# Mixture-of-experts rows sorted by single expert, or by pair of experts

## What is computed

```python
logits = einsum('bsd,de->bse', input, Wg)          # input is layernorm(x)
top_vals, top_idx = top_k(softmax(logits), 2)
top_vals = top_vals / sum(top_vals)
h = relu(einsum('ebsd,edh->ebsh', xm, W1) + b1)    # 8 experts, 128 -> 256
y = einsum('ebsh,ehd->ebsd', h, W2) + b2           # 256 -> 128
out = sum over the token's two experts of y * its share
x = x + layernorm(out)
```

## Time and profile before

| | |
|---|---|
| median of 3 runs | 952.27 us |
| profiled execution | 948.08 us |
| its span, first to last instruction | 946.2 us |
| busy: PE, DVE, ACT, POOL | 779.7, 751.3, 684.6, 581.6 us |
| mean granted TensorE clock | 0.938 |

### The profile page before, as it was taken

The page is one execution under the profiler, slowest core; times in us unless marked ns, Lnnn a source line. Parts: engine busy times, 40 slices in busy tenths (PEclk is TensorE's granted clock), DMA queues, the critical chain, the costliest instruction groups (busy, mean ns, idle before and its releaser), DMA issues.

```text
span 946.2 us, 24562 instructions
## 1 busy us (share of the span) xinstructions
PE 779.7 (82%) x7544; PEld 647.1 (68%) x7544; DVE 751.3 (79%) x2293; ACT 684.6 (72%) x1596; POOL 581.6 (61%) x832
## 2 busy tenths in 40 slices
PE   3699999999999999999999999986784798848700
PEld 2487877877877777777777777765774687738600
DVE  5677879898998989989899899977854565647876
ACT  4678888887887778877888778752663597739744
POOL 4344434376766757666676666665777777777722
PEclk9999999999999999999999999996797899989955
DMA  7000000000000000000000000062232543364643
GB/s 203 18 2 5 4 3 5 3 18 18 16 18 16 19 16 16 19 18 17 16 20 16 18 17 18 18 170 68 82 90 77 140 110 100 96 207 126 170 134 116
DMA packets 64817, 53.04 MB, mean 56 GB/s; under 512 B 11127, under 2 KB 58515, under 8 KB 64688
## 3 DMA queue, kind: packets, MB, share of 16 engines
q1 hardware_dynamic: 55600, 34.40, 13.5%
q0 software_dynamic: 9088, 17.07, 5.6%
HBM read 26.70 MB, written 25.50 MB: 55 GB/s over the span
## 4 chain that ended last, share of the span: by engine, by line
PE 48%; DVE 16%; issue 10%; ACT 7%; DMA 7%; SPq 5%; POOL 5%; DVEq 1%; POOLq 0%; ACTq 0%
PE bank L859 6%; PE bank L656 5%; PE bank L931 4%; PE bank L658 4%; PE bank L657 4%; POOL expert_results L2025 3%; PE bank L843 3%; PE bank L845 3%; PE bank L914 2%; PE bank L877 2%; PE bank L920 2%; DMA expert_results<-moe_y,moe_dest 2%; SPq L1654 2%; DMA rows<-csplit 2%; PE bank L870 2%
## 5 line engine op out<-in xcount | busy, mean ns | idle before, releaser
L2025 POOL DMA_INDIRECT expert_results<-moe_y,moe_dest x156 | 157.6, 1010 | 49.8 <-issue 42.9
L1305 POOL DMA_INDIRECT expert_rows<-xall,row_index x128 | 138.7, 1084 | 30.9 <-issue 25.3
L1020 POOL TENSOR_TENSOR y<-y,zt 128x256 f32<-128x256 f32 x64 | 46.8, 731 | 140.2 <-issue 88.7
L943 ACT ACTIVATE m<-bank 128x512 f32<-128x512 f32 x128 | 69.2, 592 | 71.6 <-PE bank L845 71.6
L2000 PE MATMUL bank<-moe_w,moe_hid 128*128 x624 | 93.5, 297 | 30.7 <-DVE moe_y L2018 22.3
L656 PE MATMUL bank<-thi,whi 128*128 128x512 f32 x224 | 105.1, 469 | 8.5 <-ACT bt L697 4.4
L2000 PEld LDWEIGHTS bank<-moe_w,moe_hid 128*128 128x128 f32 x624 | 82.3, 205 | 37.5 <-issue 36.2
L1029 DVE TENSOR_TENSOR mg<-bank,m 128x512 f32<-128x512 f32 x128 | 82.4, 685 | 19.8 <-PE bank L859 19.1
L658 PE MATMUL bank<-thi,wlo 128*128 128x512 f32 x224 | 89.7, 401 | 0.0
L657 PE MATMUL bank<-tlo,whi 128*128 128x512 f32 x224 | 89.5, 400 | 0.0
L982 POOL TENSOR_TENSOR ysum<-ysq 128x128 f32<-128x128 f32 x64 | 35.6, 556 | 71.2 <-ACT ysq L966 71.2
(11 more groups left out here) (235 smaller groups left out, 2395.0 us busy)
## 6 DMA issues: line engine op xcount, KB each, us to landing
moe_block_in<-expert_rows SPq DMA_DIRECT2D x78, 132.0 KB, 2.2
rows<-expert_results SPq DMA_DIRECT2D x12, 512.0 KB, 5.1
out_dram<-m SPq DMA_DIRECT2D x16, 256.0 KB, 2.3
expert_results<-moe_y,moe_dest POOLq DMA_INDIRECT x156
expert_rows<-spare_row SPq DMA_DIRECT2D x18, 132.0 KB, 2.8
parts<-csplit SPq DMA_DIRECT2D x128, 4.0 KB
rows<-csplit SPq DMA_DIRECT2D x128, 4.0 KB
expert_rows<-xall,row_index POOLq DMA_INDIRECT x128, 2.5
```

Source lines behind the costliest of these rows:

```text
L943: SE.activation(m[:, hf * HH:(hf + 1) * HH, :], banks[2 + hf][:].rearrange("p (h l) -> p h l", l=P), ACT.Exp).then_inc(m_ready.sem, 1)
L1305: PL.indirect_dma_start(buckets[n], bass.IndirectOffsetOnAxis(row_index[:, k, t:t + 1], 0), xall[:, t, :], None).then_inc(scattered[n], 16)
L2025: PL.indirect_dma_start(back_d, bass.IndirectOffsetOnAxis(dest[:, b % BACK, n:n + 1], 0), yout[:, b % BACK, n, :], None, bounds_check=2 * ...
```

## The change

Each token's row goes once to a bucket of its *pair* of experts (28 pairs). A unit is 128 rows of one pair; both experts are computed on it, mixed, normalised, and added to x, and one finished row per token is written to the output by an indirect DMA. There are 91 units instead of 78 blocks of 256 rows, and no last pass. The first 20 units hold rows of groups 0 to 11 only (`SPLIT = 12`, `EARLY = 20`) and run beside the last groups' routing; a unit past the end of a pair takes rows again, and those are not written twice (`again`, `skip`).

For W1 a table of both experts' columns for each of 28 pairs (and one spare) is written to DRAM during groups 3 to 10; each unit loads its 128 x 516 floats. The products with W1 are plain float32 of 128 columns without the split in two parts.

```diff
-BLK = 2 * P
-SPLIT = 11
+NPAIR = NE * (NE - 1) // 2
+SPLIT = 12
+UNITS = (TOK + NPAIR * (P - 1)) // P                                      # 91
+EARLY = -(-(SPLIT * GT - NPAIR * (P - 1)) // P) // 4 * 4                  # 20
...
 def dve_route_second(dve, q):
-        DVE.tensor_tensor(chosen[:, 1], ranks, wide(rank2[:]), ALU.is_equal)
+        DVE.tensor_tensor(upper, rank1, rank2, ALU.max)
+        DVE.tensor_tensor(lower, rank1, rank2, ALU.min)
+        DVE.scalar_tensor_tensor(out=product, in0=upper, scalar=-1.0, in1=upper, op0=ALU.add, op1=ALU.mult)
+        DVE.scalar_tensor_tensor(out=number, in0=product, scalar=0.5, in1=lower, op0=ALU.mult, op1=ALU.add)
...
-        DVE.tensor_tensor(count16[:, :, 1:TG + 1].rearrange("p e t -> p t e"), chosen[:, 0], chosen[:, 1], ALU.add)
+        DVE.tensor_tensor(marks, pair_number ... [P, TG, NPAIR], number ... [P, TG, NPAIR], ALU.is_equal)
         DVE.tensor_tensor_scan(total16, chain16, count16, ...)            # 28 x 5 columns, was 8 x 5
 def dve_route_index(dve, q):
-        DVE.tensor_tensor(spot[:], chosen[:], at.to_broadcast([P, 2, TG, NE]), ALU.mult)
-            DVE.tensor_reduce(row_index[:, :, group(q)], spot[:], AX, ALU.add)
+        DVE.tensor_tensor(spot[:], count16[:, :, 1:TG + 1], at, ALU.mult)  # 28 x 4 columns
+        DVE.tensor_reduce(place[:], spot[:].rearrange("p e t -> p t e"), AX, ALU.add)
+        DVE.scalar_tensor_tensor(out=row_index[:, group(q)], in0=pair[:, 3, :], scalar=float(BUCKET), in1=place[:], ...)
+def pool_gap(pl, q):                      # 4 POOL instructions on 128x4, once a group, ahead of the first scatter
...
 def pool_body(...):
-        for q, n in plan("scatter", g, i):
-            pool_scatter(pl, q, n, 1)
+        if isinstance(t, int) and t == 8:
+            pool_pair_b1(pl)                                              # 15 small instructions
 def pool_tail(pl, step):                  # scatters at steps 0, 1, 6, 10 (were 0, 0, 2, 5)
 def sync_program(sp):
             for u in range(GB):
                 row_copies(sp, b, u)
+                sp_pair_weights(sp, (b - 1) * GB + u)
-        for rows_d in buckets:
-            sp.dma_start(rows_d[NE * BUCKET:NE * BUCKET + BLK].rearrange("(n p) c -> p n c", p=P), dummy[:])
+        for n in range(NPAIR + 1):
+            sp.dma_start(rows_d[n * BUCKET:n * BUCKET + P], dummy[:]).then_inc(spare_rows, 16)
...
     def act_prepare(act):
         act.wait_ge(loaded, LOADS)
-        SE.activation(w1[:, :, 0, :], w1f[:], ACT.Copy)
+        SE.activation(b2x[:], b2[:], ACT.Copy).then_inc(b2_act.sem, 1)
+        act.wait_ge(b2_dve.sem, 2)
+        SE.activation(b2x[64:P, :], b2[64:P, :], ACT.Copy).then_inc(b2_act.sem, 1)
+        act.wait_ge(b2_dve.sem, 3)
+        SE.activation(b2p[:].rearrange("p e d -> p (e d)"), b2[:], ACT.Copy).then_inc(b2_act.sem, 1)
     def dve_prepare(dve):                 # two differences of 1,024 columns, a wait, a third one
...
+    def pe_up(pe, u):
+        for n in range(2 * FB):
+            mm = PE.matmul(up_at(u)[:, col(n)], w1c[:, u % WR, col(n)], ht[:, (u // 2) % HT, col(u % 2)], ...)
+    def act_hidden(act, u):               # even units: 4 activations of 128 columns; dve_hidden: odd units
+    def pe_down(pe, u):
+        for k, e in enumerate(chosen.pop(u)):
+            o = down_at(u)[:, col(k)]
+            PE.matmul(o, thirds[:], b2p[:, bass.ds(e, 1), :] ..., start=True, stop=False)     # bfloat16: the bias
+            for n in range(FB):
+                mm = PE.matmul(o, hid[:, u % HID, k, n, :], w2[:, bass.ds(e, 1), n, :] ..., stop=n == FB - 1)
+    def dve_mix(dve, u):
+        DVE.tensor_scalar(y[:, u % YR, :], o[:, col(0)], w[:, 0, i:i + 1], None, ALU.mult)
+        DVE.scalar_tensor_tensor(out=y[:, u % YR, :], in0=o[:, col(1)], scalar=w[:, 1, i:i + 1], in1=y[:, u % YR, :], ...)
+        DVE.bn_stats(st6[:, u % YR, :], y[:, u % YR, :])
+        DVE.bn_aggr(mv[:, u % YR, :], st6[:, u % YR, :])
+    def pool_out(pl, u):
+        pl.wait_ge(normed.sem, normed.of(u))
+        PL.tensor_tensor(y[:, u % YR, :], y[:, u % YR, :], block_in[:, u % IN, 0:D], ALU.add).then_inc(added.sem, 1)
+        pl.wait_ge(added.sem, added.of(u))
+        PL.indirect_dma_start(rows_out, bass.IndirectOffsetOnAxis(token[:, u % IN:u % IN + 1], 0), y[:, u % YR, :], ...)
...
     def sync_program(sp):
+            for u in units[0:ROWS_AHEAD]:                                 # 5
+                sp_load(sp, u)                                            # 128 rows, start from the table
+            for u in units:
+                if u + ROWS_AHEAD in units:
+                    sp_load(sp, u + ROWS_AHEAD)
+                sp_pick(sp, u)                                            # 128 x 516 floats of the pair
     def gpsimd_program(pl):
+        for u in range(UNITS + NORM_LAG):                                 # NORM_LAG = 7
+            if u % 4 == 3 ...: pool_shares(pl, u // 4 + 1)                # 5 small instructions for 4 units
+            if u % 4 == 1 ...: pool_share_sums(pl, u // 4)                # 2
+            if u >= NORM_LAG:
+                pool_out(pl, u - NORM_LAG)
```

More of the change, by code:

```diff
@@ L376, in fr_uses @@
         for i in range(TG):
-            seq += [made(key) for key in EARLY[i]]
+            seq += [made(key) for key in SOON[i]]
             if g is not None:
@@ L1848, in after, with unit_of, dve_table @@
+    def unit_of(u):
+        return (0, u) if u < EARLY else (1, u - EARLY)
+    def dve_table(dve, n, half):
+        rows_of = att.rows_of[:, n, :]
+        pair_number, first_row = att.pair_number[:], att.first_row[:]
+        pid, first, wanted, low, high, product, lower, taken1, start, seen = [one[:, k:k + 1] for k in range(10)]
+        at = table_i[n]
         def after(step):
             dve.wait_ge(table.sem, table.of(n, step))
-        if part == 0:
+        if half == 0:
+            dve.wait_ge(att.rows_counted.sem, n + 1)
@@ new lines, in dve_table @@
+            if n == 0:
+                DVE.memset(begun[:], 0.0).then_inc(table.sem, 1)
+            after(5)
+            DVE.tensor_tensor_scan(ends[:], att.ones[:, 0:NPAIR], unit_rows[:], 0.0, ALU.mult, ALU.add
+                                   ).then_inc(table.sem, 1)
+            after(6)
+            DVE.tensor_scalar(past[:], ends[:], first_row, None, ALU.is_le).then_inc(table.sem, 1)
+            after(7)
+            DVE.tensor_reduce(pid, past[:], AX, ALU.add).then_inc(table.sem, 1)
@@ new lines, in dve_table @@
+            DVE.tensor_tensor(past[:], past[:], unit_rows[:], ALU.mult).then_inc(table.sem, 1)
+            after(9)
+            DVE.tensor_reduce(first, past[:], AX, ALU.add).then_inc(table.sem, 1)
+            DVE.tensor_scalar(mine[:], pair_number, pid, None, ALU.is_equal).then_inc(table.sem, 1)
+            after(11)
+            DVE.tensor_tensor(past[:], mine[:], taken[:], ALU.mult).then_inc(table.sem, 1)
+            after(12)
+            DVE.tensor_reduce(taken1, past[:], AX, ALU.add).then_inc(table.sem, 1)
@@ new lines, in dve_table @@
+            DVE.tensor_tensor(mine[:], mine[:], rows_of, ALU.mult).then_inc(table.sem, 1)
+            return
+        after(14)
+        DVE.tensor_reduce(high, mine[:], AX, ALU.add).then_inc(table.sem, 1)
+        DVE.scalar_tensor_tensor(out=wanted, in0=first_row, scalar=first, in1=taken1, op0=ALU.subtract, op1=ALU.add
+                                 ).then_inc(table.sem, 1)
+        DVE.tensor_scalar(tri_past[:], att.triangle[:], pid, None, ALU.is_le).then_inc(table.sem, 1)
+        after(16)
@@ new lines, in dve_table @@
+        DVE.tensor_scalar(wanted, wanted, float(P), None, ALU.add).then_inc(table.sem, 1)
+        DVE.tensor_scalar(high, high, -float(P), 0.0, ALU.add, ALU.max).then_inc(table.sem, 1)
+        after(19)
+        DVE.tensor_tensor(start, wanted, high, ALU.min).then_inc(table.sem, 1)
+        DVE.tensor_reduce(low, tri_past[:], AX, ALU.add).then_inc(table.sem, 1)
+        after(20)
+        DVE.scalar_tensor_tensor(out=at[:, 0:1], in0=pid, scalar=float(BUCKET), in1=start, op0=ALU.mult, op1=ALU.add
+                                 ).then_inc(table.sem, 1)
@@ L1981, in act_hidden @@
[L1981 to L1994 removed]
+        wait_picked(pe, u)
@@ new lines, in vector_program @@
+    def vector_program(dve):
+        dve_skip(dve, 0)
+        for u in range(UNITS + 4):
+            if u < UNITS:
+                att.dve_tail(dve, u)
+            if u in (11, 12):
+                dve_table(dve, 1, u - 11)
+            if u == 13:
+                dve_skip(dve, 1)
+            if u in COEF_AT:
+                dve_coef(dve, COEF_AT[u])
+            if u < UNITS and u % 2:
+                dve_hidden(dve, u)
+            if 2 <= u < UNITS + 2:
+                dve_mix(dve, u - 2)
+                if u - 2 in SPREAD_AT:
+                    dve_spread(dve, SPREAD_AT[u - 2])
```

1008 lines of the change are left out of this document (501 added, 507 removed).

## The result

The changed kernel takes **987.08 us** (median of 4 runs, 986.36 to 989.48) against 952.17 for the kernel before (4 runs): 1.0372 times as long, 95% interval 1.0353 to 1.0392. The forecast of 932, and its range to 962, were wrong. The profiled execution has a span of 987.6 us, where I had 926.5: 61.1 us to explain.

A forecast was written before the change was run, and what follows sets the result against it. It took TensorE to set the attention stage's pace, VectorE close behind, and GpSimd to bound the expert stage. Last pass -33, expert stage +3, 11 lost ahead: -19.7 from 952.3, forecast 932 us, range 905 to 962.

The forecast's parts named there:

- GpSimd's unit: Expert stage, GpSimd's work per unit: one indirect DMA 1.29, add 0.45, own wait 0.1, small steps 0.43, sum 2.27 us.
- 0.1 for its own wait: Expert stage, part of GpSimd's sum per unit: 0.1 us for its wait for its own step.
- The 2.4 per unit: Expert stage: 2.4 us per unit, between 2.15 (TensorE alone) and 2.27 + 0.5 for a late neighbour; 78 units make 187.
- Attention stage: Attention groups: +0.15 us each, between -0.6 and +1.2, over 13 groups: +2 us (-8 to +16).
- the forecast's +1.4: Attention stage: about +1.4 us of VectorE per group from added routing steps, longer scan and comparison, and the index.
- The relief by the missing scatters: Attention stage: four of eight scatters go, giving 0.8 us back per group, less four tiny GpSimd steps.
- the rival that rests on it: Attention stage: the routing costs its full VectorE work, +14 us, 946 us in all; chance 0.07.
- The head: Program start: eight more small loads, with 15 small GpSimd steps in tile 8, have idle time around them: 0, at most 2 us.
- The last group: End of attention: 29 spare-row DMAs (13.8 us) ahead of the weights' loads delay ScalarE's and VectorE's preparation: +9 us.
- The first units: First 13 units beside the last routing: 42.3 us as before, two units at 2.4, 5 for the longer table: 52.
- The end: After the unit loop: GpSimd drains seven units in 13 us, last landing and last unit's chain take 3.5 more.
- VectorE as the bound: Expert stage rival: VectorE, stretched by GpSimd, needs 3.0 us per unit, 47 us more, 979 us; chance 0.20.

The follow-up runs named there:

- The seven extra steps: Kernel before with seven chained VectorE operations of 128x4 elements put behind the running sum of each group's routing, results unchanged: 969.07 us, 1.0203.
- the late return: Changed kernel with each unit's return DMA issued one unit later, behind the next unit's add: 958.81 us, 1.0088 against the kernel before.

## Why the prediction was wrong

- **GpSimd's unit (the step that failed).** The term was "0.1 for its own wait". Together with the 0.28 of issue in the 1.29 per DMA that is 0.38 us ahead of the DMA, and 0.80 us pass there. No row stood behind the 0.1, and none could: the trace before has no GpSimd DMA behind a GpSimd operation that it waits for. The real sum is 1.01 + 0.80 + 0.46 + 0.43 = 2.70 instead of 2.27: 23.7 us in the loop, and 2.27 instead of 1.84 per unit in the drain, 3 us more. Taking the wait out gave back 28. With 0.80 in its place the same sum gives about 959 us, at the edge of the range to 962, so any second miss was enough to leave it.
- **The 2.4 per unit** came out at 2.39 without the wait, but in part by luck. It was a margin on 2.27 of GpSimd and 2.15 of TensorE; with the wait gone GpSimd is far from full, and TensorE, whose 2.15 was right (2.12 at full pace), loses 0.27 per unit in small delays.
- **Attention stage.** I took +0.15 per group from a range up to +1.2; it was the upper end: 12.7 us in groups 4 to 14, 0.9 in group 3. I had called TensorE (95%) the pace and VectorE (92%) a near second. But behind its wait for TensorE's scores in the first tile (0.93 to 1.09 us before, 0.39 to 0.78 after), VectorE has no gap over 0.04 us until the running sum of the decays in the fourth, and that decides when the split of the decays is done, for which the next group waits: a share of 92% hid a chain with little slack. The seven extra steps in the kernel before show that work in this chain counts. In group 8 VectorE reaches the running sum 31.13 us behind the group's start instead of 29.74. That these 1.39 are the forecast's +1.4 is luck, since they are made up otherwise. The routing's second part and the index cost 0.40 each, and its first part takes 0.31 less. The largest piece, 0.83, stands in five normalisation steps that the change does not touch (before, then after, then GpSimd beside them after):

```profile
346.65 1.38 DVE L1108 TENSOR_SCALAR ob<-ob,pmv,pt 128x128 f32<-128x128 f32 x4
348.06 1.28 DVE L1112 TENSOR_TENSOR xall<-ob,xall 128x512 f32<-128x512 f32 x1
```

```profile
355.77 2.38 DVE L1126 TENSOR_SCALAR ob<-ob,pmv,pt 128x128 f32<-128x128 f32 x4
358.18 1.12 DVE L1130 TENSOR_TENSOR xall<-ob,xall 128x512 f32<-128x512 f32 x1
```

```profile
357.33 0.60 POOL L1022 TENSOR_TENSOR decayed<-state,edec 128x256 f32<-128x256 f32 x1
358.03 0.71 POOL L1031 TENSOR_TENSOR zt<-zsig,zt 128x256 f32<-128x256 f32 x1
```

- **The relief by the missing scatters** did come, and was lost again. One reading of the earlier trace rows was wrong: what stands beside the counting step of 0.78 us (399.00 to 399.78) is not the scatter, which has ended, but GpSimd's gate product behind it:

```profile
397.85 1.04 POOL L1305 DMA_INDIRECT expert_rows<-xall,row_index  x1 [0.15 <-DVE mtop L1264]
398.91 0.76 POOL L1013 TENSOR_TENSOR zt<-m,zt 128x256 f32<-128x256 f32 x1
```

  A scatter only decides where that product falls. After the change the counting step is stretched no longer (0.48 us, as in the groups without scatters), nor is one step of the routing's first part (0.19 instead of 0.51), and the split's second step takes 0.69 instead of 0.96. In their place another routing step takes 0.66 instead of 0.19, and the normalisation loses its 0.83. The passage of the prediction that said so, the gate product blocks VectorE just as well where it moves to, was right, and the rival that rests on it got 7 in 100.
- **The head.** 2.8 us of the profiled execution ahead of group 0 and 0.9 in it are spread between executions.
- **The last group.** +9 forecast, +11.8 measured: SyncE's 29 DMAs took 15.5 instead of 13.8 us. The mechanism was right: of the 11.8 us 8.7 came back when they went earlier, and 6.8 of the whole time.
- **The first units** took 63.8 us instead of 54. The routing steps took 47.2 instead of 42.3 us (first normalisation to the last row index). Behind them TensorE waits 4.16 us for the last step of VectorE's second table:

```profile
745.81 0.70 PE L1934 MATMUL bank<-moe_again,ones 128*128 128x71 f32 x2 [4.16 <-DVE moe_again L2028]
```

  A read of six blocks takes 10.56 us against the 6.19 of the earlier trace rows, but it starts at 751.45, 1.8 us before unit 6 is returned, and so does not explain this stretch. No experiment took it apart; it stays open. The stretch was as long in the kernel with the late return (63.9 us).
- **The end.** 9.1 us pass between the last DMA and the end of the program, in every traced kernel of the changed form; I had 3.5 for that and the last unit's chain. What they wait for stays open. Most of the rest of the 9.2 is the drain.
- **VectorE as the bound** did not come: 66% busy in the loop, and with another add per unit on it (77% busy) a unit took 2.43 us, hardly more than the 2.39 of the late return.

## What to carry to other kernels

An engine that issues a DMA on what it has just computed pays for the hand-over to itself: put the next unit's work between the two. Price a wait from a row with that very pair of instructions, and where there is none, let the range reach to the dearest wait in sight. Ask of an engine at 92% in which stretch it has no gap at all, and what lies behind that stretch: there an added microsecond counts, and a saved one may be lost again if a step moves beside another engine's. And when a sum comes out right, compare the two timelines step by step: here 1.39 us matched the 1.4 forecast, and most of it stood in steps that nobody had changed.

## What was not expected of the hardware

- A GpSimd indirect DMA that waits for the GpSimd operation issued right before it starts 0.79 to 0.82 us after that ends (79 of 79 waits that the profile puts down to it); with one DMA and one add in between the idle is 0.17 to 0.35 us (all but one of 91, which is 1.42).
- A VectorE step of 0.293 us took 0.69, 0.96 or 1.64 us by kernel, to within 0.04 us in all ten groups of one, by what GpSimd did beside it.
- TensorE's idle of 0.30 us at a group's start left the clock alone, and so did the 0.53 to 0.56 of the kernel before. 1.05 to 1.36 us were followed, in five of the nine groups from 5 to 13 in one kernel and in two of nine in another, by 3.4 or 6.8 us at a granted clock of 0.50.
